# A new order of weaving for the attention streams and the two early streams of a hybrid block

## What is computed

```python
x = x + attention_a(layernorm(x))
x = x + ffn(layernorm(x))
x = x + mamba_b(layernorm(x))
x = x + ffn(layernorm(x))
```

```python
S = S * g
delta = (v - k @ S) * beta
S = S + outer(k, delta)
o = q @ S
```

## Time and profile before

| | |
|---|---|
| median of three runs | 2520.49 us (2516.51 to 2522.57) |
| span of the profiled execution | 2516.3 us |
| time of its own beside the span | the page gives none; the shortest run is 0.2 us above the span |
| TensorE busy | 2261.4 us, 90% |
| VectorE busy | 1972.7 us, 78% |
| ScalarE busy | 1721.0 us, 68% |
| GpSimd busy | 1264.2 us, 50% |
| mean granted TensorE clock | 0.967 of full speed |
| instructions | 87483 |
| first phase | 0 to about 1840 us |

### The profile page before, as it was taken

The page is one execution under the profiler, slowest core; times in us unless marked ns, Lnnn a source line. Parts: engine busy times, 40 slices in busy tenths (PEclk is TensorE's granted clock), DMA queues, the critical chain, the costliest instruction groups (busy, mean ns, idle before and its releaser), DMA issues.

```text
span 2516.3 us, 87483 instructions
## 1 busy us (share of the span) xinstructions
PE 2261.4 (90%) x38320; PEld 1331.3 (53%) x38320; DVE 1972.7 (78%) x3031; ACT 1721.0 (68%) x3490; POOL 1264.2 (50%) x1004
## 2 busy tenths in 40 slices
PE   6689999999999999999999999998768877888777
PEld 3456666666666666666665666666423322323223
DVE  3768888888888887877887878887358789898981
ACT  2667788778887787777776778786655757656532
POOL 0445554555455444544443445553045587867960
PEclk8899999999999999999999999999879999999889
DMA  1000000000000000000000000001063062534400
GB/s 59 23 10 14 14 14 24 13 14 14 19 19 13 13 14 24 20 20 20 20 20 19 20 20 24 14 6 28 22 176 67 31 142 56 118 67 101 101 30 9
DMA packets 49837, 91.10 MB, mean 36 GB/s; under 512 B 7980, under 2 KB 17964, under 8 KB 48944
## 3 DMA queue, kind: packets, MB, share of 16 engines
q1 hardware_dynamic: 49456, 85.50, 13.1%
HBM read 74.71 MB, written 10.76 MB: 34 GB/s over the span
## 4 chain that ended last, share of the span: by engine, by line
PE 53%; DVE 19%; ACT 11%; issue 9%; POOL 6%; DMA 1%; SPq 1%; POOLq 0%; DVEq 0%; ACTq 0%
PE bank L396 9%; PE bank L500 5%; PE pair L623 4%; DVE cv L708 4%; PE bank L467 4%; PE bank L657 3%; PE pair L611 3%; POOL dBu L2289 3%; PE bank L593 2%; DVE bank L1921 2%; PE bank L436 2%; ACT Y L1084 2%; DVE kq L796 2%; PE bank L616 2%; PE pair L1587 2%
## 5 line engine op out<-in xcount | busy, mean ns | idle before, releaser
L708 DVE SCALAR_TENSOR_TENSOR cv<-raw,taps,cv 128x1024 f32<-128x1024 f32 x288 | 395.0, 1372 | 20.0 <-ACT cv L972 18.2
L396 PE MATMUL bank<-xn,W 128*128 128x512 f32 x768 | 370.7, 613 | 0.0
L1245 POOL TENSOR_TENSOR R<-kq,gate 128x1024 f32<-128x1024 f32 x32 | 77.6, 2424 | 494.2 <-ACT gate L1038 494.2
L2289 POOL TENSOR_TENSOR dBu<-dtu_wide,Bn 128x1024 f32<-128x1024 f32 x128 | 301.9, 2375 | 45.8 <-DVE bank L1921 26.5
L1268 POOL TENSOR_TENSOR kq<-kq,tot 128x512 f32<-128x512 f32 x128 | 220.2, 1720 | 206.4 <-PE bank L467 206.4
L2175 ACT ACTIVATE bank<-dt_wide,m_A 128x512 f32<-128x512 f32 x256 | 172.5, 687 | 109.5 <-DVE hc L1929 72.3
L396 PEld LDWEIGHTS bank<-xn,W 128*128 128x128 f32 x768 | 135.6, 193 | 120.7 <-issue 112.2
L971 ACT ACTIVATE raw<-bank 128x512 f32<-128x512 f32 x192 | 114.9, 598 | 94.6 <-PE bank L396 91.9
L1270 POOL TENSOR_TENSOR R<-R,tot 128x512 f32<-128x512 f32 x128 | 164.4, 1284 | 0.0
L623 PE MATMUL pair<-vT,kT 64*128 64x128 f32 x1024 | 126.3, 323 | 28.6 <-DVE vT L885 28.6
L467 PE MATMUL bank<-R,kq 128*32 128x64 f32 (+1 forms) x10240 | 134.0, 204 | 15.3 <-POOL R L1270 8.1
(11 more groups left out here) (305 smaller groups left out, 5677.3 us busy)
## 6 DMA issues: line engine op xcount, KB each, us to landing
dt_wide<-ssm_wide SPq DMA_DIRECT2D x60, 256.0 KB, 4.9
dtu_wide<-ssm_wide SPq DMA_DIRECT2D x60, 256.0 KB, 7.9
W<-in_head_w SPq DMA_DIRECT2D x32, 448.0 KB, 3.6
WO<-in_out_w SPq DMA_DIRECT2D x32, 192.0 KB, 2.4
ssm_wide<-hfa SPq DMA_DIRECT2D x8, 512.0 KB, 2.8
ssm_wide<-vc SPq DMA_DIRECT2D x8, 512.0 KB, 2.9
Bn<-ssm_rows SPq DMA_DIRECT2D x64, 64.0 KB, 5.3
Cn<-ssm_rows SPq DMA_DIRECT2D x64, 64.0 KB, 4.2
```

What stands on the lines that cost most here:

```text
L396: m = pe.matmul(psum[bank][:, :], w[:, (kind * KT + k) * P:(kind * KT + k + 1) * P], xn[:, k, b, cols], start=k == 0, stop=k == KT - 1)
L708: dve.scalar_tensor_tensor(cv[m % 2][:, :, :], raw[m % 2][:, :, i:i + SEG], taps[:, h, KQV[n], i:i + 1], cv[m % 2][:, :, :], MUL, ADD).the ...
L2289: pool.tensor_tensor(dBu[at % AHEAD][:, :, :], dtu_wide[n % 2][:, half * DT2:(half + 1) * DT2, :], spread(Bn[sg][:, :], 1, DT2), MUL).then ...
```

## The change

Only the tables change. `PLACES` gets other places for the 13 stages, with another lag for turn_v (0 becomes 1, so its steps go from 86.34 and 89.35 to 125.81 and 136.03 of the same head). `EARLY_AT` gets other places for the two early streams. `FRONT_AT` and `FFN_AT` are rounded to two decimals. Places within one row are in ascending order in both versions. The work, the tiles, the waits and the number of steps are the same.

```diff
 PLACES = [
-    (-1, [62.44, 98.25, 98.25, 107.3, 135.23, 144.87]),
-    (0, [8.7, 38.71, 40.58, 49.64, 55.51, 60.66]),
-    (0, [46.77, 46.77, 61.32, 64.82, 65.54, 66.08]),
-    (0, [65.56, 71.92, 71.92, 72.19, 84.93]),
-    (0, [47.5, 61.8, 73.89, 83.72, 83.72, 93.96, 333.79]),
-    (0, [86.34, 89.35]),
-    (0, [96.58, 99.71, 100.59, 104.48, 116.43, 118.99, 122.58, 124.72, 129.91, 130.88, 140.52, 141.22, 153.68,
-         162.41, 168.11]),
-    (1, [42.3, 60.65, 60.65, 62.21, 62.21, 65.62, 67.04, 74.72, 74.72, 82.78, 82.78, 91.21, 92.95, 95.8, 95.8]),
-    (1, [68.57, 77.03, 97.9, 132.56]),
-    (1, [99.81, 99.81, 105.11]),
-    (2, [25.65, 36.92]),
-    (2, [12.89, 15.54, 17.92, 19.58, 22.27, 22.65, 29.17, 29.17, 29.86, 39.41, 41.39, 50.71, 61.49, 67.69, 72.95,
-         79.26, 92.19, 92.19]),
-    (2, [31.85, 33.45, 94.43, 96.18, 96.23, 98.81, 102.29, 114.71, 117.96, 120.1, 170.62, 178.19, 183.69]),
+    (-1, [65.13, 94.95, 100.76, 107.99, 130.08, 138.28]),
+    (0, [13.55, 36.07, 53.05, 53.25, 54.55, 58.32]),
+    (0, [45.89, 47.33, 62.33, 62.33, 76.32, 87.22]),
+    (0, [69.0, 72.62, 92.06, 97.54, 106.8]),
+    (0, [63.45, 63.45, 63.45, 67.78, 81.33, 89.34, 226.99]),
+    (1, [25.81, 36.03]),
+    (0, [93.77, 93.77, 108.71, 111.52, 118.42, 121.99, 124.52, 128.31, 130.11, 130.11, 143.19, 143.2, 157.21,
+     176.57, 176.58]),
+    (1, [47.65, 49.27, 53.09, 58.98, 62.14, 65.28, 65.28, 70.51, 70.51, 73.38, 73.38, 86.37, 88.93, 88.93,
+     90.59]),
+    (1, [90.67, 90.67, 111.99, 118.7]),
+    (2, [2.66, 2.66, 7.99]),
+    (2, [27.5, 28.36]),
+    (2, [15.63, 17.73, 18.66, 20.19, 24.07, 25.14, 29.06, 30.65, 30.65, 37.17, 43.35, 54.41, 59.19, 66.91,
+     70.97, 80.4, 87.98, 87.98]),
+    (2, [34.29, 35.31, 93.0, 93.19, 95.31, 98.19, 108.59, 117.25, 120.68, 123.1, 161.03, 184.58, 184.58]),
 ]
 FRONT_STEPS, FFN_STEPS = 44, 26
 FRONT_AT = [
-    [131.2355, 132.8791, 132.8791, 135.1998, 135.1998, 139.2887, 139.2887, 141.9285, 142.2719, 143.6525, 143.6525,
 ...
+    [131.24, 132.88, 132.88, 135.2, 135.2, 139.29, 139.29, 141.93, 142.27, 143.65, 143.65, 143.65, 145.56,
 ...
 EARLY_AT = [
-    [1969.1115, 1969.5004, 2017.1485, 2023.4918, 2046.0532, 2056.4234, 2058.8737, 2058.8737, 2058.8737, 2152.1297,
-     2152.8414, 2160.0306, 2160.4201, 2249.5316, 2251.8889, 2255.6774, 2259.3555, 2355.1511, 2358.9463, 2358.9463,
-     2358.9463, 2468.329, 2471.1325, 2471.1325, 2471.1325, 2526.9543, 2528.3653, 2528.3653, 2528.7046, 2651.4046,
-     2652.9937, 2656.0941, 2659.9552, 2721.4569, 2723.6638, 2725.1036, 2727.3685],
-    [3241.0672, 3267.1425, 3269.2199, 3274.8651, 3278.939, 3285.1994, 3293.7517, 3298.6433, 3298.6433, 3304.8561,
-     3306.7557, 3306.7557, 3306.7557, 3306.7557, 3314.3655, 3314.3655, 3314.3655, 3315.8044, 3315.8044, 3315.8044,
-     3315.8044, 3315.8044, 3317.0603, 3317.0603, 3317.0603, 3317.0603, 3317.0603, 3317.0603, 3317.0603, 3317.3321,
-     3322.9654, 3322.9654, 3325.8103, 3340.9251, 3340.9251, 3360.1803, 3371.8137, 3373.3193, 3373.3193, 3379.9209,
-     3421.6722, 3472.9965, 3708.892, 3728.7288],
+    [2014.51, 2016.39, 2026.39, 2026.39, 2041.75, 2048.31, 2048.31, 2051.23, 2056.62, 2095.21, 2095.21, 2095.21,
+     2095.88, 2214.67, 2214.67, 2216.0, 2216.0, 2314.74, 2314.74, 2317.24, 2317.24, 2415.01, 2415.01, 2417.14,
+     2417.14, 2514.9, 2514.9, 2516.93, 2516.93, 2713.82, 2713.82, 2716.39, 2716.39, 2730.5, 2730.5, 2732.08,
+     2732.08],
+    [3244.59, 3251.62, 3261.05, 3261.05, 3264.05, 3265.35, 3272.32, 3280.81, 3284.19, 3284.19, 3293.57, 3293.57,
+     3313.74, 3315.46, 3317.04, 3317.04, 3317.04, 3317.1, 3318.4, 3318.4, 3318.42, 3318.44, 3318.44, 3318.44,
+     3318.44, 3318.44, 3319.35, 3319.94, 3319.94, 3320.08, 3325.95, 3326.35, 3328.64, 3334.19, 3341.6, 3352.48,
+     3352.48, 3352.48, 3375.14, 3380.23, 3476.69, 3476.7, 3874.8, 4165.42],
 ]
```

More of the change, by code:

```diff
@@ L56 @@
 FRONT_AT = [
[12 rows of a table removed]
[12 rows of a table added]
 ]
 FFN_AT = [
[L71 to L88, removed]
-    [636.6288, 702.0995, 709.1443, 732.4097, 732.4097, 732.4097, 1006.4481, 1120.5741, 1124.4749, 1231.7709,
-     1418.051, 1430.4292, 1471.6208, 1534.0135, 1832.7042, 1947.7258, 1962.4642, 2123.1123, 2348.7175, 2385.3661,
-     2508.8804, 2508.8804, 2551.5766, 2551.5766, 2557.8501, 2580.5935],
[15 rows of a table added]
 ]
 EARLY_AT = [
[9 rows of a table removed]
[8 rows of a table added]
 ]
```

## The result

The changed kernel takes 2813.4 us (median of 4 runs, 2809.28 to 2816.17), the kernel before 2520.13 us (4 runs, 2516.51 to 2522.57). The ratio is 1.1165, with a 95% interval of 1.1149 to 1.1182: 293 us slower. The forecast was 2790 us, with a range of 2605 to 2865 us.

What follows compares the result with a forecast made beforehand. TensorE was taken as the bound: 29 heads paying 8.1 us of waits for ScalarE plus 0.8 us of clock (258 us), plus 12 us for three other heads, make 270 us on a 2516.3 us span; median 2790 us, range 2605 to 2865.

Steps and rivals of the forecast that it cites:

- TensorE is the bound, and what it waits is added: Whole kernel: TensorE idles only 1.0 us of a 50.6 us head, so every added microsecond of waiting lengthens the head.
- The loads: ScalarE, gating 3, conv(2)'s Silu and gating 5: four more table loads a head, 128 in all, 1.283 us each, 164 us.
- Where TensorE stands: TensorE's waits for ScalarE: some 3 us at inverse step 9, about 1 at L531, some 4 at L575.
- The wait term, 8.1 us: Per head, from gating's first bank to solved's copy: ScalarE's 26.4 us less TensorE's 18.3 us; low end 6.0 us.
- The clock term, 0.8 us: Per head, TensorE's lower clock after waits: 0.8 us taken, bounds nothing and 2.5 us.
- the forecast sum of 8.9 us: Cost for each of heads 2 to 30: 8.1 us of waiting plus 0.8 us of clock, 258 us over 29 heads.
- The split: Of the 8.1 us a head, 5.2 is the loads; 2.9, or 84 us over 29 heads, is the closer order.
- dense stretch: From gating's second Abs and Relu to solved's first copy: ScalarE busy 19.18 of 20.51 us, 1.3 us to spare.
- Moves with one answer: turn_v, GpSimd's products, SyncE's weight loads, early FFN, second phase and phase end: nothing added for any beyond turn_v's counted cover.
- Loads hidden: Rival: extra loads absent or hidden, only the closer order costs, 84 us, 2605 us; chance 0.12.
- The rival of the falling clock: Rival: TensorE's clock falls to its lower level after each wait, 5 us a head more, 2912 us; chance 0.05.
- the faster case: Rival: the order fits ScalarE's free time and TensorE's 1.0 us of idle a head goes, 2490 us; chance 0.07.

Runs made afterwards that it cites:

- e4: Changed kernel with 14 extra 128x128 matmuls, later overwritten, in TensorE's wait ahead of solved step 2's second bank: 2753.9 us, ratio 1.0924.
- e1: Changed kernel with gating's Exp, Ln and Exp replaced by Tanh, so three table loads a head and other gate values: 2732.1 us, ratio 1.0837.
- e2: Kernel before with four more table loads a head, a preload pair ahead of gating step 3 and another ahead of step 5: 2683.2 us, ratio 1.0643.
- e10: Changed kernel with dots step 3 (97.54 to 103.0) and output step 5 (298.19 to 303.1) moved behind the copies of solved: 2712.4 us, ratio 1.0783.
- e11: Changed kernel with the edits of e1 and e10 together: 2627.3 us, ratio 1.0425.
- e7: Changed kernel with dots steps 2 to 4 and gating steps 3 to 5 re-placed for three table loads a head: 2844.8 us, ratio 1.1296.
- e9: Changed kernel with LN_EXP preload moved to gating 3 and 5, e10's moves, and two output products between short matmul groups: 2683.4 us, ratio 1.0668.

## Why the prediction was right, and where it was not

**TensorE is the bound, and what it waits is added.** Right. A head went from 50.6 to 60.1 us for the forecast 59.5. All that the order gained is the 1.0 us a head of the old idle time.

**The loads.** Right in number (four a head, 128 in all), place and length (1.283 us, ScalarE 164 us longer). Behind the load of L990, which starts at 683.67 us and takes 1.28 us, the next activation starts at 684.97 us (its row stands above): nothing lies between them here either.

**Where TensorE stands.** Right in place: inverse step 9 behind the UM copy, and L569 behind the copy of solved. Forecast were 3, 1 and 4 us at L494, L525 and L569; measured are 2.0, 0.04 and 3.5.

**The wait term, 8.1 us.** Oversized: TensorE's idle time grew by 5.2 us a head. Two things were left out. The sum kept the 1.0 us a head that TensorE waited at L623 before, and the new order has none of it. And it took the 18.3 us of TensorE's queue at full clock, while in the changed kernel part of it runs at the lower level: two output products take 3.52 or 3.78 us there for 1.98 in e4. With the rows around them that is some 1.8 us a head, and it fills the wait at L525: in the head at 661 us TensorE starts the product of Z 0.3 us after the copy has ended, so by my estimate it would have waited 1.2 us without the 1.5 us of slow rows, about as forecast. 8.1 - 1.0 - 1.8 = 5.3 us. The balance itself was good: from the end of gating's first bank (660.7 us) to the copy of solved (686.5) ScalarE took 25.8 us for 26.4.

**The clock term, 0.8 us.** Undersized: 4.3 us a head, a mean of 0.91, beyond the 0.95 that I had taken as the worst. Some 1.8 us of it stand in the place of a wait, as just told; the other 2.5 us are L569 and L461 behind the wait at L569 (3.68 for 2.00 and 1.93 for 1.10), and they are added. e4 shows the same, since 60 us come back when that wait is filled. So the forecast sum of 8.9 us met the measured 9.5 with one term too large and the other too small, which is partly luck.

**The split, "5.2 us is the loads; 2.9 us would be there without them".** Wrong. The order alone costs 211 us (e1), for which the split gives 84; the loads alone cost 162 us in the old order (e2), and together they cost 293 us. They are not terms of a sum: each fills waits that the other makes. The step that failed was to set one balance over the whole dense stretch. TensorE has several appointments with ScalarE in it, and each has a balance of its own. In e1 ScalarE works from the end of the copy of Z (780.88 us) to the end of the first copy of solved (789.01) with hardly a pause, 8.1 us with one load among it. TensorE starts the product of Z 0.6 us after the copy and has 5.3 us of rows up to L569. That leaves 2.3 us at L569, whatever happened earlier. In the changed kernel one of the four loads more lies in between, and all five waits of the middle window are 3.53 us. e10 and e11 took 2.3 us of ScalarE's work out of this piece: 101 and 105 us. What I had not priced at all are the stops inside the short groups, 2.2 us a head in the middle of e1 and 59 us in all.

**Moves with one answer.** Beside the early stream the head's time rose by 8.4 us for 9.5 us in the middle. From GpSimd's products step 0 of the first head to that of the last are 1631.7 us before and 1914.2 after, 282 of the 293 us; ahead of it lie 2 us more and behind it 9 us more, which I had taken as nothing.

**Rivals.** "Loads hidden" fell with the 128 loads in the changed profile and with e2; its price for the closer order, 84 us, was far too low (e1: 211). The rival of the falling clock was nearer than its chance of 0.05: the clock did fall after each wait, for 4.3 us a head, near its price of 5 us, only the waits were smaller. What the faster case rested on, TensorE's own 1.0 us of idle time, did go away, but the waits for ScalarE are six times as long.

**What is open.** The stops inside the groups are stops for instructions. The profile's page has a queue of its own for them ("q8 instruction: 303, 4.96", packets and MB, so 16 KB each), and the traces hold 77584 instructions of TensorE (38320 matmuls, 38320 weight loads and 944 that only wait): one packet for 256 instructions. Counted through, all 438 stops of over 0.1 us inside a group, in the 13 traces of this case, stand at the same place when the records are counted in blocks of 256 (number 193 or 194 from 0), and 436 of them end 1.2 to 1.6 us after a packet of q8 has landed. In e1 one packet starts at 772.09 us and takes 1.34 us, and TensorE goes on at 774.88. The 3.5 us at L569 are of another kind: their place in the block moves on by one from head to head and the wait stays the same, so they are ScalarE's. How fast the blocks come is seen where two stops follow each other: the two restarts lie 3.3 to 4.0 us apart in e1, e7 and e11 (68 pairs), for a block that gives TensorE 2.07 us of work in this window of e1:

```profile
770.96:774.88 3.92, 2.07 (x129) 1.70 (x128) 1.69 (x5) 2.00 (x6) 0.00 (x0) 1.00 0.02 4
```

In the kernel before, products of 1 us, which need few instructions, stand between the groups. No run changed the supply itself, and why a block takes that long is not shown. Nor is it settled which steps make the last 168 us of e9.

## What to carry to other kernels

In woven code an engine with a third of its time free can still set the time: look for the stretch where it is solid, and set up the balance between each two appointments with the bound engine, not over the stretch or the kernel. A function that needs other tables costs little in a slack stretch (11 us for 128 loads) and about its own length in a dense one (162 us for 164 us of loads in the old order); after a reorder, list the activations in their new order and count the loads. Where TensorE is the bound, a wait can cost twice: the matmuls behind the waits of 1.8 to 3.5 us ran at the lower clock here, those behind the 1.2 us of e10 did not. Long runs of short matmuls want long ones between them, or TensorE stops for its own instructions.

## What the runs showed of the hardware that was not expected

- The clock falls after single waits of 1.8 to 3.5 us in a TensorE that is otherwise busy: rows behind them take 3.68 for 2.00 us. With 3.4 us of useless matmuls in the wait they take 2.00 us, and the kernel is 60 us faster.
- TensorE can stand still for 1.9 us (e1), once for 2.7 us (e7), inside a group of short matmuls without a semaphore, where five groups of 64 follow each other closely; in the kernel before, with 1 us products between them, this window had none. All such stops stand at one place of a block of 256 instructions, and where they follow each other the blocks come 3.3 to 4.0 us apart.
- A wait that the profile puts down to "issue" (L569) can be one for ScalarE: the copy ended 0.1 us before, and moving 2.3 us of ScalarE's work took 2.3 us from it.
